# Releasing GpSimd's weight splits at VectorE's peak reductions, and moving weight blocks, transposes and small scale operations in a two-layer adaLN and FFN kernel

## The chip, the cores and the metric

One Trainium2 chip (trn2), one of its cores. The metric is the device time of one execution, in microseconds (us), lower is better. The engines are TensorE (PE in the views), VectorE (DVE), ScalarE (ACT), GpSimd (POOL) and SyncE (SP), which here only issues DMAs.

## The reference

The input `x` has 16 batches of 128 x 128 floats. Two layers are added to it, each a conditioning followed by an FFN. Cut to what matters:

```
# layer 0, conditioning: one 128x128 matrix for each batch, applied to x
w = scale * weight * y[:, None, :];  w = w * rsqrt(sum(w*w) + 1e-8);  c = einsum('boi,bil->bol', w, E)
# layer 0, FFN with quantised activations (each act_qdq needs the largest absolute value of its whole tensor)
act_qdq(x): s = max(max|x| / 32767, 1e-12);  clip(round(x / s), ...) * s
x = act_qdq(c);  up = act_qdq(x @ dq(w_up).T);  gate = act_qdq(x @ dq(w_gate).T)
sig = fixed_qdq_u16(sigmoid(gate));  gate = act_qdq(gate * sig);  o = act_qdq(gate * up);  return o @ dq(w_down).T
# layer 1, conditioning: a recurrence over 128 time steps
next_h = tanh(x_t @ Wx + b + prev_h @ Wh)
# layer 1, FFN: 8 experts of 512 hidden units with exact gelu, the best 2 of them mixed by a softmax
```

The two layers follow each other, so layer 1 cannot start before layer 0 has its result.

## The kernel before

The program is written by hand: each engine has its own list of instructions, and semaphores tie the lists together. Nothing is scheduled by a planner; the order in the source is the order on the engine.

**Front, up to about 82 us.** VectorE and ScalarE turn five tensors into integers. Each tensor's scale is made by `peak_to_scale(i, ...)`, i from 0 to 4: c, gate, up, gate times sigmoid, and the product o. VectorE first reduces pieces of the tensor to peaks (`block_peak`, `peak_gate_up`), then these to one column (`pk1`, semaphore `pk_part`). TensorE spreads that column over all partitions (`spread_peak`, a matmul with the identity into bank 7, semaphore `pk_all`). VectorE takes the maximum (`pkm`), the reciprocal and the scale (semaphore `scale_done`). While the spread runs, VectorE prepares the scale's limits: `unit` writes column 0 of `sc`, L708 writes it divided by QMAX, and L709 divided by TINY; then it does what the argument `meanwhile` names.

- The sigmoid stage (L825 to L833) works in six pieces of 1024 columns. ScalarE quantises a piece of gate (L596), takes the sigmoid (L600), and from the third piece on rounds it to 16 bits (L603); VectorE rounds the first two itself (`round_sigmoid`, L810), multiplies (L829, semaphore `g2_done`) and reduces (L723).
- The product stage (L836 to L845) has six pieces too. VectorE quantises the first (L836), ScalarE the others (L614, semaphore `g2q`) and up in three parts (L607, `upq`). VectorE multiplies (L841, `p_done`) and reduces (L723).
- `take_xT` on ScalarE evicts the transposes of `x` that TensorE makes at L1074.

**The experts' weights** are 16 chunks of 128 x 512 floats (`W_CHUNKS`). Each has to be scaled, split into a high and a low half-precision part, and transposed. The first `W_POOL` = 8 are split by GpSimd (`split_weights`, L375 to L377: scale, high part, difference), and SyncE transposes both parts by DMA (L335). For the other 8, ScalarE writes the high part (`weight_hi`, L535) and SyncE transposes it (L338), while TensorE makes the low part: for each chunk a **weight block** of four pairs of matmuls (L1092 to L1095) that ScalarE evicts (`weight_lo`, L540). There are eight chunk buffers for 16 chunks, so chunk 8 and later ones wait for the first eight transposes (semaphore `wt_t[0]`). GpSimd also dequantises the three FFN weights (`scale_weights`, L384 to L387), and splits the router weights, the recurrence's bias, the experts' second bias (`split_b2`) and Wh (`split_wh`).

`keep_busy(WARM)` gives TensorE 14 matmuls whose result nobody reads, ahead of the weight blocks. The spread for scale 4 stands ahead of the last two blocks (L1086).

**Middle, about 82 to 98 us.** `quantise_o` on VectorE, the down projection in five column chunks (`WIDTHS`) on TensorE, and the first 16 recurrence steps.

**Experts, about 98 us to the end.** TensorE runs the expert matmuls and the rest of the recurrence between them, chunk by chunk. `input_part` prepares `x_t @ Wx` for the next chunk's steps. The bias `b` enters in one of two ways: before chunk `BIAS_FROM` = 2 by one more matmul (`bh_rows` x `ones`), from that chunk on as the bias operand of the tanh (L663 to L666). Chunks 2 and 3 take two tanh for each step, chunk 2 in 32 steps and chunk 3 in 24.

## Time and profile before

| | |
|---|---|
| median of 3 executions | 293.2 us (292.99 to 293.34) |
| the profiled execution, its own time | 293.86 us |
| its span, first to last instruction | 292.1 us |
| busy: PE / DVE / ACT / POOL | 258.1 / 257.5 / 218.5 / 91.9 us |
| mean granted TensorE clock | 0.953 of full speed |

How to read it: the span is counted from the first instruction and leaves out 1.8 us around it. Every duration used below comes from this one profiled execution. Two engines have nearly the same busy time, so the shares of the whole say little; the stages have to be read one by one.

### The profile page before, as it was taken

What the parts mean: (1) busy time and instruction counts of PE and PEld (TensorE: products, weight loads), DVE (VectorE), ACT (ScalarE), POOL (GpSimd) and SP (SyncE); (2) the same over time, 40 slices, a digit from 0 to 9 for tenths busy, and PEclk for the clock granted to TensorE, in tenths of its full rate; (3) what the DMA queues carried; (4) which work ended last, traced back from release to release, by engine and by line L of the source; (5) the groups of instructions that cost most, each with busy time, mean ns of one, the idle gap of its engine ahead of it and who ended that gap; (6) DMA issues with size and microseconds to landing.
All of it is one profiled execution on the core that took longest, in us unless ns stands there. A gap on an engine that the chain in (4) does not pass through costs nothing.

```text
span 292.1 us, 7662 instructions
## 1 busy us (share of the span) xinstructions
PE 258.1 (88%) x2828; PEld 196.1 (67%) x2828; DVE 257.5 (88%) x638; ACT 218.5 (75%) x510; POOL 91.9 (31%) x181
## 2 busy tenths in 40 slices
PE   4999850039999999999999999999999999999994
PEld 3843450016866889888888676767677777778774
DVE  4899999989999999979988799778799988899885
ACT  5487899998742677777777777787678777788992
POOL 3539999250036413113212213333211232201000
PEclk9999957558999999999999999999999999999999
DMA  6992343001400000000000000000001000001001
GB/s 172 325 333 47 72 95 72 15 0 36 92 18 2 1 2 2 3 0 21 2 0 3 2 5 25 2 2 3 1 2 38 3 0 2 3 2 37 0 2 29
DMA packets 24041, 10.77 MB, mean 37 GB/s; under 512 B 13355, under 2 KB 22982, under 8 KB 24006
## 3 DMA queue, kind: packets, MB, share of 16 engines
q1 hardware_dynamic: 23470, 10.05, 13.7%
q8 instruction: 22, 0.36, 0.6%
q10 hardware_dynamic: 536, 0.26, 0.3%
q14 instruction: 13, 0.11, 0.1%
HBM read 6.11 MB, written 1.05 MB: 25 GB/s over the span
## 4 chain that ended last, share of the span: by engine, by line
PE 69%; DVE 24%; DMA 3%; issue 2%; ACT 1%; POOL 0%; SPq 0%; DVEq 0%
PE bank L998 68%; DVE peak L723 6%; DVE peak L805 4%; DVE big L829 3%; DVE big L841 3%; DMA wn<-in_w_gate 2%; DVE q L795 1%; DVE big L810 1%; DMA y_sb<-in_cond 1%; PE bank L1124 1%; DVE ws L750 1%; DVE big L836 1%; DVE big L849 1%; DVE big L977 0%; DVE pkm L712 0%
## 5 line engine op out<-in xcount | busy, mean ns | idle before, releaser
L998 PE MATMUL bank<-big,wt 128*128 128x384 f16 (+2 forms) x480 | 123.1, 336 | 0.0
L998 PE MATMUL bank<-wt,big 128*128 128x128 f16 (+1 forms) x1536 | 110.8, 219 | 0.2 <-DVE big L977 0.2
L998 PEld LDWEIGHTS bank<-wt,big 128*128 128x128 f16 x1536 | 98.2, 97 | 15.9 <-DVE big L977 0.5
L977 DVE TENSOR_TENSOR big<-big 128x384 f16<-128x384 f32 (+2 forms) x160 | 93.1, 587 | 17.7 <-ACT big L679 13.2
L677 ACT ACTIVATE big<-bank,miscT 128x384 f32<-128x384 f32 (+2 forms) x160 | 96.5, 604 | 10.3 <-PE bank L998 9.4
L998 PEld LDWEIGHTS bank<-big,wt 128*128 128x128 f16 (+1 forms) x480 | 44.8, 107 | 3.8 <-issue 0.2
L459 POOL TENSOR_TENSOR big<-q,big 128x16 f16<-128x16 f32 x56 | 23.5, 419 | 66.6 <-ACT q L666 66.6
L973 DVE CAST big<-big 128x512 f16<-128x512 f32 (+2 forms) x104 | 38.7, 372 | 4.0 <-ACT big L677 3.5
L932 DVE SCALAR_TENSOR_TENSOR wyT<-bank,gates,wyT 128x128 f32<-128x128 f32 x128 | 39.7, 343 | 0.3 <-issue 0.2
L679 ACT ACTIVATE big<-bank,miscT 128x384 f16<-128x384 f32 (+2 forms) x56 | 33.1, 592 | 0.0
L665 ACT ACTIVATE big<-bank,miscT 128x16 f16<-128x16 f32 x56 | 15.4, 276 | 18.1 <-PE bank L998 17.9
L998 PEld LDWEIGHTS bank<-q,wxh 128*128 128x128 f32 x142 | 23.6, 190 | 5.1 <-ACT q L637 1.2
L998 PE MATMUL bank<-q,wxh 128*128 128x16 f32 x142 | 21.3, 226 | 0.3 <-ACT q L637 0.3
L450 POOL CAST big<-q 128x64 f16<-128x64 f32 x18 | 6.6, 367 | 47.2 <-ACT q L666 46.9
L998 PE MATMUL bank<-ident,pk 128*128 128x128 f32 x10 | 2.9, 383 | 20.4 <-DVE pk L706 20.4
L666 ACT ACTIVATE q<-bank 128x16 f32<-128x16 f32 x56 | 10.3, 184 | 12.9 <-PE bank L998 12.5
L998 PEld LDWEIGHTS bank<-big,wh_hi 128*128 128x128 f16 x112 | 10.0, 96 | 12.9 <-POOL big L459 9.4
L998 PEld LDWEIGHTS bank<-ident,pk 128*128 128x128 f32 x10 | 2.0, 237 | 21.9 <-DVE pk L706 16.8
L586 ACT ACTIVATE big<-bank 128x512 f32<-128x512 f32 x24 | 13.4, 612 | 2.6 <-PE bank L998 2.3
L998 PE MATMUL bank<-q,wT_hi 128*128 128x512 f16 x48 | 15.1, 380 | 0.1
L666 ACT ACTIVATE q<-bank,miscT 128x16 f32<-128x16 f32 x56 | 15.1, 270 | 0.0
L723 DVE TENSOR_REDUCE peak<-big 128x1 f32<-128x1024 f32 x12 | 14.6, 1220 | 0.4
(177 smaller groups left out, 386.1 us busy)
## 6 DMA issues: line engine op xcount, KB each, us to landing
wnat<-in_w SPq DMA_DIRECT2D x8, 512.0 KB, 7.6
x_sb<-in_x SPq DMA_DIRECT2D x4, 256.0 KB, 4.1
out_block<-wyT SPq DMA_DIRECT2D x15, 64.0 KB
wn<-in_w_gate ACTq DMA_DIRECT2D x1, 192.0 KB, 5.4
wn<-in_w_up SPq DMA_DIRECT2D x1, 192.0 KB, 5.5
wn<-in_w_down SPq DMA_DIRECT2D x1, 192.0 KB, 5.5
b_in<-in_b SPq DMA_DIRECT2D x12, 4.0 KB
wt<-wyT SPq DMA_TRANSPOSE x8, 3.0
```

The source lines that it names most:

```text
L459: G.tensor_tensor(h_lo[:, at], h32[:, at], h_hi[:, at], ALU.subtract).then_inc(h_lo_done, 1)
L586: A(blk(t, j * NK + k), banks[GU_BANKS[n % 5]][:, :], ACT.Copy).then_inc(gu_sb, 1)
L665: A(h_hi[:, bass.ds(step * B, B)], sums, ACT.Tanh, bias=bias, scale=1 / WS).then_inc(h_hi_s, 1)
L666: A(h32[:, bass.ds(step * B, B)], sums, ACT.Tanh, bias=bias, scale=1 / WS).then_inc(h32_done, 1)
L677: A(g32[:, f, 0:w], ps_h[f][:, 0:w], ACT.Gelu, bias=bias, scale=1 / WS).then_inc(g32_done, 1)
L679: A(g_hi[:, s // NF, f, 0:w], ps_h[f][:, 0:w], ACT.Gelu, bias=bias, scale=1 / WS).then_inc(g_hi_done, 1)
L723: link(V.tensor_reduce(peak[:, i, n:n + 1], t, X, ALU.max, apply_absolute_value=True))
L805: link(V.tensor_reduce(peak[:, i, k:k + 1], tokens((gate2, up2)[i - 1], k), XY, ALU.max, apply_absolute_value=True))
L932: V.scalar_tensor_tensor(a, ps_y[par][:, P * j:P * (j + 1)], g, a, ALU.mult, ALU.add).then_inc(added, 1)
L973: V.tensor_copy(g_hi[:, par, f, 0:w], g32[:, f, 0:w]).then_inc(hi_v, 1)
L977: V.tensor_tensor(g_lo[:, par, f, 0:w], g32[:, f, 0:w], g_hi[:, par, f, 0:w], ALU.subtract).then_inc(g_lo_done, 1)
L998: return nc.tensor.matmul(o, l, r, start=start, stop=stop, skip_group_check=True)
```

## The change

Twelve edits in one. They are numbered here, and the prediction speaks of them by these names.

- **Limits.** `peak_to_scale` writes its two limits directly from two numbers (two operations instead of three), for scales 1, 3 and 4. Scale 0 takes them from a constant tile `limits` that GpSimd fills at the start, scale 2 from scale 1, both with no operation of VectorE.
- **Splits behind.** GpSimd's chunks 5, 6, 7 wait for VectorE's products: `split_behind(i, made, n)` starts after product n (n = 0: at once) and its last operation after product n+1. `scale_weights(1)` waits for `q_done`, the router weights for `g2_done` 6, the bias for `p_done` 1, `split_b2` for `p_done` 6 and its last operation for `pk_part` 5.
- **Two chunks moved.** Chunks 8 and 9 go from ScalarE and TensorE to GpSimd (`W_POOL` 10, `W_FIRST` 8), behind products 2 to 5 of the product stage; SyncE transposes them last, in full.
- **ScalarE's order.** Two quantised pieces before the table load, the others between weight parts; `low_byte(0)` ahead of the last two low parts.
- **Early transposes.** Two of the four transposes of `x` (8 of 16 matmuls, and 2 evictions) move to the start.
- **Spreads.** Spread 0 goes ahead of the transposes of the gate weights; spread 4 comes after the last weight block and two more warming matmuls. `WARM` 14 to 4, `START_WARM` 3 to 2.
- **wT_lo of down.** `weight_lo(2)` moves on VectorE from the peaks of up into the wait for spread 3.
- **upq.** Product n waits for the third of up that it reads, no longer for all three.
- **Bias.** `BIAS_FROM` 3: chunk 2's tanh has no bias operand, and chunk 1's `input_part` for those steps one more matmul of 512 columns.

```diff
-W_POOL = 8
+W_POOL = 10
+W_FIRST = 8
+X_EARLY = (6, 5)
+X_LATE = (1, 2)
-WARM = 14
+WARM = 4
+LATE_WARM = 2
-BIAS_FROM = 2
+BIAS_FROM = 3
-START_WARM = 3
+START_WARM = 2
...
+            def split_behind(i, made, n):
+                src, hi, lo = wnat[:, i % 2, i // 2, :], nat_of(i)[:, 0:FF], nat_of(i)[:, FF:2 * FF]
+                if n:
+                    pool.wait_ge(made, n)
+                link(G.tensor_scalar(src, src, WS, 0.0, ALU.mult, ALU.add))
+                link(G.tensor_scalar(hi, src, 1.0, 0.0, ALU.mult, ALU.add))
+                pool.wait_ge(made, n + 1)
+                G.tensor_tensor(lo, src, hi, ALU.subtract).then_inc(nat_done, 1)
...
+            pool.wait_ge(q_done, NK)
             scale_weights(1)
...
-            split_weights(POOL_FIRST, W_POOL)
+            split_weights(POOL_FIRST, W_FIRST - 3)
+            split_behind(W_FIRST - 3, g2_done, 0)
+            split_behind(W_FIRST - 2, g2_done, 2)
+            split_behind(W_FIRST - 1, g2_done, 4)
...
+            pool.wait_ge(wt_t[0], 16 * W_FIRST)
+            split_behind(W_FIRST, p_done, 2)
+            split_behind(W_FIRST + 1, p_done, 4)
             split_b2()
...
-                unit(sc[:, i, 0:1])
-                link(V.tensor_scalar(sc[:, i, 1:2], sc[:, i, 0:1], 1.0 / QMAX, None, ALU.mult))
-                link(V.tensor_scalar(sc[:, i, 5:6], sc[:, i, 0:1], 1.0 / TINY, None, ALU.mult))
+                for a, limit in enumerate((1.0 / QMAX, 1.0 / TINY) if unit else ()):
+                    link(V.tensor_scalar(sc[:, i, a:a + 1], unit[0], unit[1], limit, ALU.mult, ALU.mult))
...
-            dve.wait_ge(upq, NJ)
             for n in range(2 * NJ):
+                dve.wait_ge(upq, n // 2 + 1)
...
             for i in range(W_POOL, W_CHUNKS):
-                if i == W_CHUNKS - 2:
-                    spread_peak(4)
...
                 last.then_inc(w_lo_mm, 1)
+            keep_busy(LATE_WARM)
+            spread_peak(4)
```

How the order moves, at the two places on which the largest terms rest. First GpSimd from its sixth chunk (number 5) on, through the sigmoid and the product stage. `wnat` is a chunk as loaded, `nat` and `wyT` hold its two parts. Before:

```order
L375 TENSOR_SCALAR wnat<-wnat 128x512
L376 TENSOR_SCALAR nat<-wnat 128x512 [waits pool_step]
L377 TENSOR_TENSOR nat<-wnat,nat 128x512 [waits pool_step]
L406 TENSOR_SCALAR rw<-miscT 128x8 [waits misc_sb]
...
L421 TENSOR_SCALAR b2_in<-b2_in 96x512 [waits pk_part,ld_b2,bh_ready]
```

and now:

```order
L412 TENSOR_SCALAR wnat<-wnat 128x512 [waits g2_done]
L413 TENSOR_SCALAR nat<-wnat 128x512 [waits pool_step]
L415 TENSOR_TENSOR nat<-wnat,nat 128x512 [waits g2_done,pool_step]
L432 TENSOR_SCALAR rw<-miscT 128x8 [waits g2_done,misc_sb]
...
L412 TENSOR_SCALAR wnat<-wnat 128x512 [waits ld_w2,p_done,wt_t0,bh_ready]
L413 TENSOR_SCALAR wyT<-wnat 128x512 [waits pool_step]
L415 TENSOR_TENSOR wyT<-wnat,wyT 128x512 [waits p_done,pool_step]
...
L448 TENSOR_SCALAR b2_in<-b2_in 96x512 [waits p_done,ld_b2]
```

Each chunk's first and third operation now carry a wait for VectorE, and two chunks are new. Second, ScalarE in the product stage: `big<-big,sc` is a quantised piece, `xT` an evicted transpose, `wyT<-wnat` and `nat<-wnat` a high part, `wt<-bank` a low part. Before:

```order
L608 ACT_TABLE_LOAD
L546 ACTIVATE xT<-bank 128x512 [waits xT_mm] x2
L614 ACTIVATE big<-big,sc 128x1024 [waits scale_done]
...
L614 ACTIVATE big<-big,sc 128x1024 x3
L535 ACTIVATE wyT<-wnat 128x512 [waits ld_w2,wt_t0]
```

and now:

```order
L645 ACTIVATE big<-big,sc 128x1024 [waits scale_done]
L645 ACTIVATE big<-big,sc 128x1024
L649 ACT_TABLE_LOAD
L566 ACTIVATE wyT<-wnat 128x512 [waits ld_w2,wt_t0]
L566 ACTIVATE wyT<-wnat 128x512 [waits ld_w2]
L577 ACTIVATE xT<-bank 128x512 [waits xT_mm]
L645 ACTIVATE big<-big,sc 128x1024
L571 ACTIVATE wt<-bank 128x512 [waits w_lo_mm]
L566 ACTIVATE nat<-wnat 128x512 [waits ld_w3]
```

The first high part now precedes three of the five quantised pieces, and these stand behind low parts, which wait for TensorE.

## Rows read from the trace of the kernel before

**Rows 1.** Chain that ended last, in time: start, length, what.

```profile
166.53 121.80 PE bank L998 x1577
```

**Rows 2.** Timeline of VectorE, 19 to 27 us: start, length, line, operation, tiles.

```profile
19.41 1.86 DVE L795 SCALAR_TENSOR_TENSOR q<-c,q 128x512 f16<-128x512 f32 x2
...
26.17 0.56 DVE L763 TENSOR_TENSOR wT_lo<-bank,wT_hi 128x384 f16<-128x384 f32 x1
```

**Rows 3.** Timeline of GpSimd, 19 to 46 us.

```profile
22.32 0.84 POOL L387 TENSOR_TENSOR wn<-wn,ws 128x384 f32<-128x384 f32 x1
...
25.76 0.83 POOL L384 TENSOR_TENSOR wn<-wn,ws 128x384 f32<-128x384 f32 x1
...
27.87 0.83 POOL L387 TENSOR_TENSOR wn<-wn,ws 128x384 f32<-128x384 f32 x1
...
44.15 1.16 POOL L377 TENSOR_TENSOR nat<-wnat,nat 128x512 f16<-128x512 f32 x1
```

**Rows 4.** Timeline of VectorE, 39 to 57 us.

```profile
39.47 0.16 DVE L706 TENSOR_REDUCE pk<-peak 128x1 f32<-128x4 f32 x1
...
40.10 0.69 DVE L810 TENSOR_SCALAR big<-big 128x1024 f32<-128x1024 f32 x1
...
44.31 1.55 DVE L810 TENSOR_SCALAR big<-big 128x1024 f32<-128x1024 f32 x1
45.89 1.51 DVE L829 TENSOR_TENSOR big<-big 128x1024 f32<-128x1024 int16 x1
...
56.52 1.22 DVE L829 TENSOR_TENSOR big<-big 128x1024 f32<-128x1024 int16 x1
```

**Rows 5.** Timeline of VectorE, 59 to 79 us.

```profile
59.03 0.16 DVE L706 TENSOR_REDUCE pk<-peak 128x1 f32<-128x6 f32 x1
...
60.15 0.29 DVE L712 TENSOR_REDUCE pkm<-bank 128x1 f32<-128x128 f32 x1 [0.52 <-PE bank L998]
...
60.92 1.55 DVE L836 TENSOR_SCALAR big<-big,sc 128x1024 f32<-128x1024 f32 x1
...
77.72 0.16 DVE L706 TENSOR_REDUCE pk<-peak 128x1 f32<-128x6 f32 x1
...
78.53 0.29 DVE L712 TENSOR_REDUCE pkm<-bank 128x1 f32<-128x128 f32 x1 [0.21 <-PE bank L998]
```

**Rows 6.** Timeline of ScalarE, 53 to 72 us.

```profile
53.26 1.34 ACT L603 ACTIVATE big<-big 128x1024 uint16<-128x1024 f32 x1
...
60.24 1.28 ACT L608 ACT_TABLE_LOAD   x1
...
65.54 3.23 ACT L614 ACTIVATE big<-big,sc 128x1024 f32<-128x1024 f32 x3
68.66 1.15 ACT L535 ACTIVATE wyT<-wnat 128x512 f16<-128x512 f32 x2
...
70.92 0.60 ACT L540 ACTIVATE wt<-bank 128x512 f16<-128x512 f32 x1 [1.11 <-PE bank L998]
```

**Rows 7.** Timeline of TensorE, 63 to 73 us (first matmul of blocks 8 and 10).

```profile
63.79 5.42 PE L998 MATMUL bank<-wT_hi 128*128 128x512 f16 x14 [3.76 <-DVE big L841]
69.34 0.49 PE L998 MATMUL bank<-ident,wnat 128*128 128x128 f32 x2
...
72.09 0.49 PE L998 MATMUL bank<-ident,wnat 128*128 128x128 f32 x2
```

**Rows 8.** Busy times by stretch: PE, PEld, DVE, ACT, POOL, then the granted clock.

```profile
37.50:38.00 0.50, 0.00 (x0) 0.00 (x0) 0.50 (x2) 0.50 (x1) 0.42 (x2) 0.60 0.76 155
...
66.00:68.00 2.00, 2.00 (x6) 0.66 (x5) 1.93 (x3) 2.00 (x3) 0.00 (x0) 0.50 0.00 0
68.00:70.00 2.00, 1.87 (x10) 0.98 (x9) 1.97 (x2) 1.81 (x3) 0.00 (x0) 0.92 0.00 0
```

**Rows 9.** Costliest groups: one tanh of a step with and without bias operand.

```profile
L666 ACT ACTIVATE q<-bank 128x16 f32<-128x16 f32 x56 | 10.3, 184 | 12.9 <-PE bank L998 12.5
...
L666 ACT ACTIVATE q<-bank,miscT 128x16 f32<-128x16 f32 x56 | 15.1, 270 | 0.0
```

More of the change, by code:

```diff
@@ L110, in program @@
         pkm = sb("pkm", [P, 5])
-        sc = sb("sc", [P, 5, 6])
+        sc = sb("sc", [P, 5, 5])
+        limits = sb("limits", [P, 2])
         x1 = c32[:, :, :].rearrange("p b l -> p (b l)")
@@ L367, in _ @@
             G.tensor_scalar(minus16[:, :], ident[:, :], -1.0 / WS, 0.0, ALU.mult, ALU.add).then_inc(consts, 1)
+            link(G.memset(limits[:, 0:1], 1.0 / QMAX))
+            G.memset(limits[:, 1:2], 1.0 / TINY).then_inc(consts, 1)
             link(G.memset(ones[:, :], 1.0))
@@ L570, in take_weights @@
                   ACT.Copy).then_inc(wT_hi_done, 1)
+            for k in range(len(X_EARLY)):
+                take_xT(k)
             take_weights(0)
@@ L607, in _, with take_g2 @@
                 A(third(up2, n), third(up2, n), ACT.Copy, scale=sc[:, 2, 4:5], bias=MAGIC).then_inc(upq, 1)
-            nc.scalar.preload_act_table(ACT.Gelu)
-            for k in range(2):
-                take_xT(k)
-            act.wait_ge(scale_done, 4)
-            for n in range(1, 2 * NJ):
-                A(sixth(sig2, n), sixth(sig2, n), ACT.Copy, scale=sc[:, 3, 4:5], bias=MAGIC).then_inc(g2q, 1)
-                if n <= 2:
-                    take_xT(n + 1)
-            act.wait_ge(wt_t[0], 16 * W_POOL)
-            weight_hi(W_POOL)
-            for i in range(W_POOL, W_CHUNKS - 1):
-                weight_hi(i + 1)
+            act.wait_ge(scale_done, 4)
+            def take_g2(n):
+                A(sixth(sig2, n), sixth(sig2, n), ACT.Copy, scale=sc[:, 3, 4:5], bias=MAGIC).then_inc(g2q, 1)
+            take_g2(1)
+            take_g2(2)
+            nc.scalar.preload_act_table(ACT.Gelu)
+            act.wait_ge(wt_t[0], 16 * W_FIRST)
+            weight_hi(W_POOL)
+            weight_hi(W_POOL + 1)
+            take_xT(2)
+            take_g2(3)
+            weight_lo(W_POOL)
+            weight_hi(W_POOL + 2)
+            take_xT(3)
+            take_g2(4)
+            weight_lo(W_POOL + 1)
+            weight_hi(W_POOL + 3)
+            take_g2(5)
+            for i in range(W_POOL + 2, W_CHUNKS - 2):
                 weight_lo(i)
+                weight_hi(i + 2)
             def low_byte(c):
@@ L627, in _ @@
             low_byte(0)
-            weight_lo(W_CHUNKS - 1)
+            for i in range(W_CHUNKS - 2, W_CHUNKS):
+                weight_lo(i)
             for c in range(1, LOW_SCALAR):
@@ L700, in _, with limits_of @@
             V = nc.vector
+            def limits_of(i):
+                own = sc[:, 1 if i == 2 else i, 0:2] if i else limits[:, :]
+                return own[:, 0:1], own[:, 1:2]
             def peak_to_scale(i, n, unit, meanwhile=lambda: None):
                 V.tensor_reduce(pk1[:, i:i + 1], peak[:, i, 0:n], X, ALU.max).then_inc(pk_part, 1)
-                unit(sc[:, i, 0:1])
-                link(V.tensor_scalar(sc[:, i, 1:2], sc[:, i, 0:1], 1.0 / QMAX, None, ALU.mult))
-                link(V.tensor_scalar(sc[:, i, 5:6], sc[:, i, 0:1], 1.0 / TINY, None, ALU.mult))
+                for a, limit in enumerate((1.0 / QMAX, 1.0 / TINY) if unit else ()):
+                    link(V.tensor_scalar(sc[:, i, a:a + 1], unit[0], unit[1], limit, ALU.mult, ALU.mult))
+                most = limits_of(i)[1]
                 meanwhile()
@@ L817, in _ @@
                         weight_lo(1)
-                    if i == 2 and k == 2:
-                        weight_lo(2)
-                peak_to_scale(i, NK, lambda u: link(V.tensor_scalar(u, sc[:, 0, 2:3], 1.0 / WS, None, ALU.mult)),
-                              (lambda: peak_gate_up(2, 0)) if i == 1 else (lambda: round_sigmoid(0)))
+                peak_to_scale(i, NK, (sc[:, 0, 2:3], 1.0 / WS) if i == 1 else None, (lambda: peak_gate_up(2, 0)) if i == 1 else (lambda: round_sigmoid(0)))
                 if i == 1:
@@ L880, in _ @@
             make_x1(CH - 1)
-            dve.wait_ge(wt_t[1], 16 * (W_CHUNKS - W_POOL))
+            dve.wait_ge(wt_t[1], 16 * (W_CHUNKS - W_FIRST))
             for k in range(ACC_SCALAR[0]):
@@ L1037, in transpose_weights, with transpose_x @@
                 last.then_inc(wT_mm, 1)
+            def transpose_x(k):
+                bank = banks[(X_EARLY + X_LATE)[k]]
+                for b in range(4 * k, 4 * k + 4):
+                    last = nc.tensor.transpose(bank[:, P * (b % 4):P * (b % 4 + 1)], x_sb[:, b, :], ident[:, :])
+                last.then_inc(xT_mm, 1)
+            for k in range(len(X_EARLY)):
+                transpose_x(k)
             for k in range(NK):
@@ L1070, in _ @@
             spread_peak(2)
+            for k in range(len(X_EARLY), NK):
+                transpose_x(k)
+            spread_peak(3)
             pe.wait_ge(wT_done, 3)
-            for k in range(NK):
-                for b in range(4 * k, 4 * k + 4):
-                    last = nc.tensor.transpose(banks[1 + k][:, P * (b % 4):P * (b % 4 + 1)], x_sb[:, b, :], ident[:, :])
-                last.then_inc(xT_mm, 1)
-            spread_peak(3)
             def keep_busy(n):
```

45 lines of the change are left out of this document (27 added, 18 removed).

## The prediction

> **What bounds the kernel now.** I read the chain of waits in time first. Before 82 us it runs almost wholly through VectorE; the experts' part is TensorE without a gap that matters, its last piece alone 121.80 us [rows 1]. So what the front gives back should come through to the end, and what frees ScalarE or VectorE in the experts' part should not. The timelines by engine then show what VectorE pays in the front beyond its own work. Its product L829 takes 1.22 us when GpSimd is idle and 1.51 when it is not, and the rounding L810 takes 0.69 or 1.55 [rows 4]. The reader should see in GpSimd's row what stood in the way: a difference that ran from 44.15 for 1.16 us, over the start of L810 at 44.31 [rows 3, 4]. L836 is the same kind of operation as L810 and also takes 1.55 [rows 5]. ScalarE and TensorE must be read beside it, since little slack is left: ScalarE's last rounding of the sigmoid stage ends at 54.60 and VectorE uses it at 56.52 [rows 4, 6].
>
> **The change, part by part.** Times are places in the execution shown.
>
> *Start.* The limits of scale 0 cost VectorE nothing now, but TensorE has eight more transposes before the spread, so I expect 0.25 us, between 0 and 0.4. Holding `scale_weights(1)` back frees VectorE's two operations at L795: they took 1.86 us together, and 1.4 would be two at the length of an undisturbed one, so 0.4 more. But GpSimd then starts at about 20.7. Its four operations take 2.94 us undisturbed (25.76 to 28.70) and so end at 23.65, where they ended at 23.16 [rows 3]. The transposes, the eviction and `weight_lo(1)` all follow GpSimd: VectorE, early by 0.6, has to wait there, and L763 ends about 0.2 later than the old 26.73 [rows 2]. The whole gain of the start is spent on this wait. TensorE and ScalarE behind it start the sigmoid stage some 0.26 us late.
>
> *Scales 1 and 2.* One limit operation less before scale 1 gives 0.19, and `weight_lo(2)` leaves the peaks of up: 0.56 [rows 2]. L706 moves from 39.47 to about 38.94. Three limit operations for scale 2 go, but then the spread is what ends last: at half clock it is 0.96 from the end of L706 to L712 (59.19 to 60.15) [rows 5]. L712 comes at 38.94 + 0.16 + 0.96 = 40.06, where it came when L810 ended, 40.79 [rows 4]. That makes 0.7 in all so far.
>
> *Sigmoid stage.* L810 loses 1.55 - 0.69 = 0.86; of the first three L829, two lose 0.29 and one 0.20: 0.78 [rows 4]. VectorE alone would reach L706 at 59.03 - 0.7 - 1.64 = 56.7. It will not, because ScalarE's last piece comes at 54.60 + 0.26 = 54.86 [rows 6]; a product and a peak of 1.22 and two gaps of 0.02 follow, and L706 starts at 57.4. **The gain is capped at 1.65 us here.** GpSimd's three chunks fit: its difference of 1.16 lies beside a peak of 1.22, and two scalings of 0.62 each overhang the peak by about 0.1.
>
> The Trainium skill (SBUF — State Buffer, Who interferes with whom) says of VectorE and GpSimd that the second to issue is fully blocked until the first ends. By that rule L810 would have ended at 45.31 + 0.69 = 46.00; the row has 45.86, so the trace agrees within 0.14. By the rule an overhang of 0.1 costs 0.1, which changes the sum by less than 0.3 over all pieces.
>
> *Scale 3 and L836.* `weight_lo(2)` (0.56) and two limit operations (0.37) fit exactly into the 0.96 of the spread; I cost them at nothing, and at 0.1 if the spread is fast. L836 loses 0.86 because `split_b2` is now behind the products. The product stage starts 1.65 + 0.86 = 2.5 us early, and VectorE alone would have L706 at 77.72 - 2.5 = 75.2 [rows 5].
>
> *ScalarE's chain in the product stage.* This is where I expect the bound. ScalarE's three L607 start when the sigmoid stage ends there, and so end at 60.24 + 0.26 = 60.50. Until the last high part it has five pieces at 1.04 (65.54 to 68.66 is three), a table load of 1.28, six high parts, four low parts and two xT, each 0.57 (two take 1.15) [rows 6]. The sum is 13.3 us. To this comes one wait: block 10 starts with the first high part at 64.4, and TensorE is then at half clock. A block takes 1.37 at full clock (69.34 to 72.09 is two) [rows 7], 2.75 at half: it ends at 67.2, and ScalarE is there at 66.6. So the last high part ends at 60.5 + 13.3 + 0.6 = 74.4. Its block takes 1.4 and the two warming matmuls 0.4, half of 0.39 (14 in 5.42 us [rows 7]) for each. TensorE is free at 76.2, and VectorE's peaks have been ready since 75.4. From the end of L706 to L712 it was 0.65 at full clock (77.88 to 78.53) [rows 5]: L712 comes at 76.8, **1.7 us early**. The pieces for VectorE are in time: the third is ready at 66.6 and wanted at 67.7, the fourth at 69.9 and 70.2, the fifth at 72.1 and 72.7.
>
> The clock rows carry this. It rose at 68.3, 4.5 us after the warming began at 63.79 [rows 7, 8]. Steady work from 64.4 on would bring it by 69, in block 11. If it rises earlier, ScalarE's wait of 0.6 goes. If it stays low for one block more, 0.5 is lost.
>
> *After L712.* The split of Wh (a cast and a difference of 128 columns) now follows `split_b2` at 76.6 and ends before VectorE's first `quantise_o` at 77.6: nothing, at most 0.7 if the scale comes earlier. SyncE's two late transposes are issued by 78 and needed at 83. Nothing else between 78.5 and the experts changes.
>
> *Experts.* A tanh without bias operand takes 184 ns, with it 270 [rows 9]. ScalarE is spared 64 x 86 ns = 5.5 us; I cost that at nothing, because TensorE is the chain there. The extra matmul of 512 columns is on TensorE: 0.2 us lost.
>
> **Sum.** -1.7 + 0.2 = -1.5 us. The profiled execution of 293.86 would become 292.4. The median shown is 0.7 lower than that execution, so the forecast for the median is 293.2 - 1.5 = **291.7 us**. Its own range, by the bounds of the start (0.4), the overhangs (0.3) and the block (0.6), is 290.9 to 292.4.
>
> **Rivals.**
>
> - *The clock comes early and VectorE holds the end.* The last spread then waits for L706 only: L712 at 75.4 + 0.65 = 76.05, 2.5 us early. But `quantise_o` would then meet the split of Wh and give back 0.3 to 0.7. Result -1.8 to -2.0 with the bias, 291.3. For it: the four warming matmuls run just ahead of the blocks. Against it: ScalarE's sum of 13.3 us alone ends at 73.8, which puts the last spread's start at 75.6. Chance 0.17.
> - *Slower: the clock falls behind the last spread.* Now TensorE has two blocks between the spread and the down projection; after the change it has nothing from 77.4 until the first `o_hi` at 78.8, then 1.3 us of work and another gap. It fell at 37.6, with TensorE idle since gate and up [rows 8]. If the matmuls from 81 us on start at half clock, it may last as long as the low stretch from 63.79 to 68.3, 4.5 us [rows 7, 8], in which half the work is done: 2.3 us lost, against 1.5 won, 0.8 slower than before, 294.0. A dip half as long gives 292.9. It decides from the point where the granted clock is 0.5 at the down projection's second chunk. Chance 0.1, half of it for the long dip.
> - *The queue behind GpSimd costs more.* A wait for a product's semaphore delays chunk 5 to 7, these delay `wt_t[0]`, and the first high part waits for it; or the clock rises a block later. Nothing in the rows shows a delay over 1 us. The gain falls to 0.6: 292.6. Chance 0.1.
> - *The table load is paid in full.* Today ScalarE has slack there; after the change the load is inside its chain, with work queued behind. If the switch holds the engine for twice the 1.28 of its row [rows 6], the gain falls by 1.3 us to 0.2: 293.0. Against it: the transposes' eviction followed this load at once. The Trainium skill (ScalarE: Activation LUTs, What ACT_TABLE_LOAD costs) states a drain of 1.38 us beside a load of 1.28. By that rule the time would be 293.1; the row shows the 1.28 and no drain. Chance 0.04.
> - *Nothing is released.* The splits could already lie beside the peaks. The rows say no: three L829, L810 and L836 are all stretched. Chance 0.02.
> - The remaining 0.57 is the forecast.
>
> **Numbers.** About 0.2% (0.6 us) is what a measurement of this kernel can tell from no change: below 292.6 is faster, above 293.8 slower. The forecast and the first rival are faster, 0.74, and a third of the rest adds 0.05: **faster 0.79**. The queue, the table load, the short dip and no release fall mostly within: **same 0.13**. The long dip, with a little for a cost that I don't see: **slower 0.08**. The range leaves out the long dip and reaches to the short one and to the first rival's lower end: 290.6 to 293.1.
>
> **What would show it right or wrong.** In the changed profile the products of the sigmoid stage should take 1.22 each and L810 and L836 0.69. There should be a new wait of VectorE for `weight_lo(1)` of about 0.8, and one for ScalarE's last sigmoid piece. L706 of scale 3 should start near 57.4, the last spread's L712 near 76.8 with TensorE, not VectorE, as what it waits for, and the clock should be at full speed from 69 on. Wrong would be: full clock before 66; a granted clock of 0.5 anywhere between 77 and 90; L712 later than 78; or an experts' part (from the first expert matmul to the end) that differs by more than 0.4 us from that of before.

## The result and the profile after

The changed kernel took **291.07 us**, the median of five executions (289.96 to 291.83), against 293.03 for the kernel before in the same comparison. The ratio is 0.9923, with a 95% interval from 0.9909 to 0.9937. The forecast was 291.7 us. Four of the five executions show a mean granted clock of TensorE of 0.941; the fifth, of 289.96, shows 0.953. That difference matters below.

| | before | after |
|---|---|---|
| profiled execution | 293.86 us | 291.07 us |
| its span | 292.1 us | 289.3 us |
| mean granted clock | 0.953 | 0.941 |
| first expert matmul | 105.89 | 104.24 |
| from there to the end of the chain's last long piece | 182.44 | 181.23 |

The chain that ended last, with the page's shares by engine first, then start, length, what:

```profile
PE 78%; ACT 13%; DVE 4%; issue 2%; POOL 1%; DMA 1%; SPq 0%; DVEq 0%; POOLq 0%
```

```profile
53.86 4.46 ACT big L640 x3
...
63.56 2.84 PE bank L1045 x12
...
72.16 3.54 PE bank L1045 x28
...
77.93 6.02 PE bank L1045 x32
...
104.24 181.23 PE bank L1045 x2344
```

VectorE has nearly left the chain. In the whole view it goes through ScalarE from 32.64 on, through all of the sigmoid stage, and from 62.88 on to and fro between ScalarE and TensorE through the weight blocks. The experts' part is one piece, where it was several [rows 1]. The timeline of VectorE in the changed kernel (start, length, line, operation, tiles, and in brackets the idle time before it and what ended that):

```profile
18.36 1.22 DVE L845 SCALAR_TENSOR_TENSOR q<-c,q 128x512 f16<-128x512 f32 x2
...
25.44 0.56 DVE L812 TENSOR_TENSOR wT_lo<-bank,wT_hi 128x384 f16<-128x384 f32 x1 [1.04 <-ACT wT_hi L600]
...
38.09 0.16 DVE L755 TENSOR_REDUCE pk<-peak 128x1 f32<-128x4 f32 x1
...
39.20 0.29 DVE L761 TENSOR_REDUCE pkm<-bank 128x1 f32<-128x128 f32 x1 [0.21 <-PE bank L1045]
...
42.65 0.69 DVE L860 TENSOR_SCALAR big<-big 128x1024 f32<-128x1024 f32 x1
43.38 1.23 DVE L876 TENSOR_TENSOR big<-big 128x1024 f32<-128x1024 int16 x1
...
53.96 1.23 DVE L876 TENSOR_TENSOR big<-big 128x1024 f32<-128x1024 int16 x1 [0.57 <-ACT big L636]
...
56.48 0.16 DVE L755 TENSOR_REDUCE pk<-peak 128x1 f32<-128x6 f32 x1
...
57.52 0.29 DVE L761 TENSOR_REDUCE pkm<-bank 128x1 f32<-128x128 f32 x1
...
58.30 0.75 DVE L883 TENSOR_SCALAR big<-big,sc 128x1024 f32<-128x1024 f32 x1
...
74.37 0.16 DVE L755 TENSOR_REDUCE pk<-peak 128x1 f32<-128x6 f32 x1
...
75.80 0.29 DVE L761 TENSOR_REDUCE pkm<-bank 128x1 f32<-128x128 f32 x1 [0.90 <-PE bank L1045]
```

Line by line these answer to [rows 2, 4, 5]: the pair of L845 1.22 instead of 1.86, the rounding of the sigmoid stage 0.69 instead of 1.55, the product behind it 1.23 instead of 1.51, L883 0.75 instead of 1.55. Two waits are new: 0.57 for ScalarE's last sigmoid piece, and 0.90 for TensorE at the last spread. GpSimd, ScalarE and TensorE in the same kernel, from their timelines:

```profile
19.67 0.83 POOL L393 TENSOR_TENSOR wn<-wn,ws 128x384 f32<-128x384 f32 x1 [5.67 <-DVE q L845]
```

```profile
61.59 1.28 ACT L649 ACT_TABLE_LOAD   x1
62.88 1.15 ACT L566 ACTIVATE wyT<-wnat 128x512 f16<-128x512 f32 x2
...
66.42 0.60 ACT L571 ACTIVATE wt<-bank 128x512 f16<-128x512 f32 x1 [0.87 <-PE bank L1045]
...
72.46 0.65 ACT L566 ACTIVATE nat<-wnat 128x512 f16<-128x512 f32 x1
```

```profile
77.93 0.49 PE L1045 MATMUL bank<-big,wT_hi 128*128 128x256 f16 x3 [2.24 <-DVE big L898]
```

TensorE stood still for 2.24 us behind the last spread. The busy times by stretch show what came of it (the stretch and its length; the busy time of PE, PEld, which is TensorE's weight loads, DVE, ACT and POOL, with the number of instructions; then the granted clock, where 0.50 is 1.2 GHz and 1.00 is 2.4 GHz; the last two columns are DMA):

```profile
68.00:70.00 2.00, 1.92 (x17) 1.65 (x15) 1.93 (x3) 2.00 (x5) 1.24 (x2) 0.98 0.33 66
...
78.00:80.00 2.00, 2.00 (x12) 1.50 (x12) 1.68 (x3) 2.00 (x4) 0.00 (x0) 0.58 0.89 167
80.00:82.00 2.00, 2.00 (x9) 1.02 (x8) 1.59 (x4) 0.15 (x1) 0.00 (x0) 0.57 0.00 0
82.00:84.00 2.00, 1.94 (x15) 1.18 (x12) 1.97 (x3) 0.21 (x2) 1.24 (x1) 1.00 0.00 0
```

The clock rose at 68.1, as expected, and fell again from about 78.3 to 81.7, in the middle of the down projection.

**Where the time went.** The five L761 (L712 before) cut the execution into stretches that don't depend on when the first load landed. That landing varies from one execution to the next: the first load of the profiled execution of before ended at 3.35, that of after at 2.89, which alone is 0.46 of the difference between the two. All numbers are differences of start times in one profiled execution of each kernel; the last column is the median of all its timed executions, with its ratio to before, which was timed again beside each group of runs (293.03 to 293.45). So kernels of different groups are compared by their ratios.

| kernel | scale 0 to 2 | 2 to 3 | 3 to 4 | scale 4 to first expert matmul | experts | median us (ratio) |
|---|---|---|---|---|---|---|
| before | 25.48 | 19.44 | 18.38 | 27.36 | 182.44 | 293.03 |
| after | 25.02 | 18.32 | 18.28 | 28.44 | 181.23 | 291.07 (0.9923) |
| b_bias3 | 25.46 | 19.45 | 18.38 | 27.37 | 181.36 | 292.38 (0.9960) |
| a_bias2 | 24.71 | 18.67 | 18.29 | 27.37 | 182.33 | 291.36 (0.9940) |
| a_fill | 24.70 | 18.63 | 18.30 | 27.36 | 181.22 | 290.10 (0.9886) |
| a_nowaits | 25.01 | 18.79 | 18.24 | 28.40 | 181.24 | 291.45 (0.9928) |
| b_behind | 25.47 | 17.83 | 21.11 | 27.38 | 182.44 | 293.71 (1.0019) |
| b_behind_warm | 25.48 | 17.82 | 19.57 | 27.37 | 182.43 | 292.62 (0.9976) |
| a_last1 | 24.71 | 18.65 | 17.65 | 27.44 | 181.23 | 289.60 (0.9871) |
| a_early | 25.01 | 18.33 | 17.65 | 28.57 | 181.22 | 291.05 (0.9924) |
| a_noq | 24.69 | 18.32 | 18.28 | 28.44 | 181.21 | 291.16 (0.9920) |
| a_last1_nowaits | 24.71 | 19.11 | 18.26 | 28.10 | 181.23 | 291.20 (0.9928) |
| a_last1_early | 25.01 | 18.33 | 17.96 | 27.77 | 181.22 | 289.70 (0.9872) |
| a_ops | 25.29 | 18.05 | 18.29 | 28.50 | 181.23 | 291.58 (0.9934) |

From before to after: -1.68 from scale 0 to scale 4 (63.30 to 61.62), +1.08 behind it, -1.21 in the experts' part. Ahead of scale 0, L755 to L761 is 0.81 (13.37 to 14.18), where it was 1.18: -0.37. The sum is -2.18; the medians differ by 1.96. The forecast had -1.7 for the front, scale 0 included, nothing for the stretch behind it, and +0.2 for the experts.

### The profile page after: what moved, and what is told of

It is laid out like the page before. It is cut to its first block, busy times and chain, and to the rows that moved or that the text cites. A ratio compares the mean times of both kernels' runs of the same rounds, so it can differ in the third digit from the quotient of the medians.

```text
span 289.3 us, 7599 instructions
## 1 busy us (share of the span) xinstructions
PE 253.0 (87%) x2795; PEld 194.5 (67%) x2795; DVE 253.9 (88%) x629; ACT 213.0 (74%) x506; POOL 91.7 (32%) x189
## 4 chain that ended last, share of the span: by engine, by line
PE 78%; ACT 13%; DVE 4%; issue 2%; POOL 1%; DMA 1%; SPq 0%; DVEq 0%; POOLq 0%
PE bank L1045 76%; ACT big L633 2%; ACT big L629 2%; ACT big L636 2%; ACT big L640 2%; ACT big L645 1%; DVE q L845 1%; PE bank L1179 1%; PE bank L1098 1%; DMA y_sb<-in_cond 1%; ACT big L619 1%; ACT wt L571 1%; ACT nat L566 1%; DVE big L1024 1%; ACT L649 0%
## 5 line engine op out<-in xcount | busy, mean ns | idle before, releaser
L490 POOL TENSOR_TENSOR big<-q,big 128x16 f16<-128x16 f32 x56 | 24.4, 436 | 64.2 <-ACT q L710 64.2
L710 ACT ACTIVATE q<-bank 128x16 f32<-128x16 f32 x88 | 16.0, 182 | 12.7 <-PE bank L1045 12.5
L709 ACT ACTIVATE big<-bank 128x16 f16<-128x16 f32 x32 | 5.9, 184 | 12.9 <-PE bank L1045 12.9
L855 DVE TENSOR_REDUCE peak<-big 128x1 f32<-128x1536 f32 x8 | 14.0, 1744 | 0.2
```

Source lines behind the costliest of these rows:

```text
L490: G.tensor_tensor(h_lo[:, at], h32[:, at], h_hi[:, at], ALU.subtract).then_inc(h_lo_done, 1)
L710: A(h32[:, bass.ds(step * B, B)], sums, ACT.Tanh, bias=bias, scale=1 / WS).then_inc(h32_done, 1)
L855: link(V.tensor_reduce(peak[:, i, k:k + 1], tokens((gate2, up2)[i - 1], k), XY, ALU.max, apply_absolute_value=True))
```

## The experiments

Every kernel is an edit of the one before or of the changed one.

**The bias operand, both ways.** a_bias2 puts it back into the changed kernel, b_bias3 takes it out of the one before.

```
-BIAS_FROM = 3
+BIAS_FROM = 2      # a_bias2; b_bias3 is 2 -> 3 in the kernel before
```

> The change with the bias operand put back in chunk 2, nothing else. Theory A, the step chain: in the experts' part of before TensorE stood 1.2 us at about 162.6 and 1.2 us at about 165.3, each ended by ScalarE's tanh and GpSimd's split of a state; the tanh without its bias operand frees ScalarE there, and this is the 1.2 us that the experts' part lost (182.48 to 181.26). Then this kernel is 1.0 to 1.4 us slower than the change, 292.3, with stalls of TensorE of about 1.2 us back some 60 us into the experts' part, and the experts' part is 182.5 again. Theory B, as forecast: TensorE is the chain, the bias is worth nothing, the matmul spared gives 0.2: 0.2 us faster than the change, 290.9, and the experts' part stays at 181.1. Theory C: the experts' part is shorter because the front hands over in another order; then also within 0.2 of the change.

> The kernel before with the bias operand taken from chunk 2, nothing else. Theory A (step chain): 1.0 to 1.4 us faster than before, 291.8, all of it after the first expert matmul. Theory B (forecast): 0.2 us slower, 293.2. Theory C (order of the handover): within 0.2 of before. If A holds, the front of the change alone is worth only about 0.7 us of the 1.96 at the end.

Measured: 291.36 (ratio 0.994, 0.9919 to 0.9961) and 292.38 (0.996, 0.9946 to 0.9974). Theory A holds in its size: the operand is the cause of the 1.2 us. The experts' part is 182.33 with it in the changed kernel and 181.36 without it in the kernel before. The theory's reading of where the 1.2 us lie, as two stops of TensorE, does not hold. The medians say the same for b_bias3, 1.07 below before's 293.45. For a_bias2 the median alone is only 0.3 above the change's, since four of its seven executions escaped the fall of the clock (0.945 to 0.953, 290.69 to 291.36) and three did not (0.940 to 0.941, 292.00 to 292.89). The chain of the kernel before, around the place (start, length, what):

```profile
162.75 0.28 ACT q L666
...
163.09 0.62 POOL big L459
...
165.83 0.66 POOL big L459
```

Twice the chain leaves TensorE for a recurrent step: a tanh for the high half, one for the full state, then GpSimd's difference, 1.2 us each time (162.56 to 163.76). TensorE does not stand still for these 1.2 us. Its timeline has other matmuls beside them, and the step's matmul at 163.76 starts 0.65 after the pair of 512 columns ahead of it, where such a pair takes 0.44 when nothing waits. The chain's hop is long, and what it costs is 0.2.

The timelines of a_bias2 and of the changed kernel can be laid side by side, matmul by matmul, with times counted from the first expert matmul. At the first input matmul behind the extra one, a_bias2 is 0.41 ahead (53.53 against 53.94): this is the price of the extra matmul. Behind the second hop it is 0.07 ahead (60.50 against 60.57), so the two hops together are worth 0.34. At 203.62 in its timeline it is 1.11 behind (100.21 against 99.10), and stays there. Most of the loss, 1.18, thus comes in 24 us of the long piece that the chain shows as unbroken TensorE. The weight loads (PEld) show what it is, first in a_bias2, then in the changed kernel:

```profile
163.91 0.10 PEld L1045 LDWEIGHTS bank<-big,wh_hi 128*128 128x128 f16 x1 [0.58 <-POOL big L490]
...
179.97 0.10 PEld L1045 LDWEIGHTS bank<-big,wh_hi 128*128 128x128 f16 x1 [0.48 <-POOL big L490]
...
203.61 0.10 PEld L1045 LDWEIGHTS bank<-big,wh_hi 128*128 128x128 f16 x1 [0.48 <-POOL big L490]
```

```profile
182.06 0.10 PEld L1045 LDWEIGHTS bank<-big,wh_hi 128*128 128x128 f16 x1 [0.31 <-POOL big L490]
...
201.88 0.10 PEld L1045 LDWEIGHTS bank<-big,wh_hi 128*128 128x128 f16 x1 [0.29 <-POOL big L490]
```

From 179.97 to 203.61 a_bias2 has nine weight loads that wait 0.39 to 0.48 for GpSimd's difference, and its matmuls fall behind by 0.07 to 0.20 at each of them. In the changed kernel no wait between 178 and 203 is longer than 0.31. The view of L459 (L490) by who waited for it adds the waits up, in us and times, before and after:

```profile
  PEld bank L998: 9.4, 27
```

```profile
  PEld bank L1045: 5.0, 17
```

Of these 4.4 us, about 1.5 reach the end. The kernel before and b_bias3, laid side by side, differ in the same way: 0.41 for the extra matmul, 0.34 at the two hops, 1.14 behind them.

**Filling TensorE's gap behind the last spread.** a_fill:

```
             keep_busy(LATE_WARM)
             spread_peak(4)
+            keep_busy(9)
```

> The change with nine warming matmuls behind the last spread, on TensorE's idle time from 75.7 to 77.9. Theory D: the granted clock falls at 78.3 because TensorE stands still behind the last spread, and the half clock from 78.3 to 81.7 costs 1.1 us (the spread's L712 was 2.7 us early, the first step only 1.66). Nine matmuls of 0.22 fill 1.9 of the 2.2 us, the clock stays full, and the kernel is 1.0 to 1.2 us faster than the change, 290.0, with a mean granted clock of 0.953 instead of 0.941. Rival E: the gain is lost elsewhere between the spread and the first step (the low bytes, VectorE's quantise and x1), and the clock dip lies beside waits: then 0 to 0.3 faster, with full clock throughout.

Measured: 290.10 (ratio 0.9886, 0.9866 to 0.9907). Theory D holds: scale 4 to the first expert matmul is 27.36, not 28.44, which is before's own 27.36. Only the mean clock was put too high (0.944 to 0.947), because in these executions it rose later, at about 70. Busy times by stretch of a_fill, columns as above:

```profile
78.00:79.00 1.00, 0.80 (x8) 0.75 (x9) 0.93 (x4) 1.00 (x3) 0.00 (x0) 1.00 0.97 185
...
80.00:81.00 1.00, 0.93 (x6) 0.60 (x7) 0.93 (x4) 0.41 (x1) 0.00 (x0) 1.00 0.00 1
```

So the fall costs 1.08 us. That is less than half of the 3.4 us from its fall to its rise. Probably part of it lies beside VectorE's own work, which no run shows alone.

The profiled execution of a_bias2 tells the fall from the gap. It has no filling and the same gap, but its clock stayed at full speed:

```profile
78.18 0.49 PE L1045 MATMUL bank<-big,wT_hi 128*128 128x256 f16 x3 [2.25 <-DVE big L898]
```

From scale 4 to the first expert matmul it takes 27.37. So the gap by itself costs nothing, and the fall of the clock is the whole 1.08.

**The last block behind the last spread.** a_last1:

```
+            for i in range(W_POOL, W_CHUNKS - 1):
+                weight_block(i)
-            keep_busy(LATE_WARM)
             spread_peak(4)
+            weight_block(W_CHUNKS - 1)
+            keep_busy(LATE_WARM)
```

> The change with the last spread ahead of the last weight block (and of the two late warming matmuls), not behind it. Theory J: the blocks ahead of the last spread cost twice: the spread waits for TensorE (L761 at 75.80 with 0.90 idle, L755 had been at 74.37), and behind it TensorE stands still for 2.2 us, which lets the clock fall for 1.07 us of loss. With one block behind the spread, L761 comes 0.65 after L755, 0.8 earlier; the block fills the gap, and the clock stays full: scale 3 to 4 falls from 18.29 to 17.5, last spread to first expert matmul from 28.44 to 27.4; the kernel is 1.6 to 1.9 us faster than the change, 289.3. Rival K: the block behind the spread delays the down projection or the low bytes, or the clock falls all the same: 0 to 0.8 faster.

Measured: 289.60 (ratio 0.9871, 0.9856 to 0.9885). Theory J, by 0.3 less than the expected 289.3. TensorE and VectorE of a_last1, from their timelines:

```profile
74.81 0.49 PE L1045 MATMUL bank<-ident,pk 128*128 128x128 f32 x2 [0.84 <-DVE pk L755]
...
77.67 0.49 PE L1045 MATMUL bank<-big,wT_hi 128*128 128x256 f16 x3 [0.66 <-DVE big L898]
```

```profile
75.41 0.29 DVE L761 TENSOR_REDUCE pkm<-bank 128x1 f32<-128x128 f32 x1 [0.28 <-PE bank L1045]
```

The spread now waits for VectorE's peak. The gap behind it is 0.66 instead of 2.24, and the clock stays at 1.00 there. This part of the change, the blocks ahead of the last spread, goes one block too far: with the last one behind it the front is 0.63 shorter and the fall of the clock is gone.

**The clock ahead of the blocks.** a_early:

```
-WARM = 4
+WARM = 14
-            pe.wait_ge(p_done, 1)
             keep_busy(WARM)
```

> The change with fourteen warming matmuls instead of four, started without the wait for the first product, so from 57.4 on. Theory L: the clock is at full speed before block 10 (at 63.5), the block takes 1.4 instead of 2.84, ScalarE's wait of 0.87 for it goes, and with it scale 3 to 4 falls by 0.6 to 0.8, to 17.6: 0.6 to 0.8 faster if the clock dip behind the last spread stays, 290.4. Rival M: the clock falls again between the warming and the blocks, or the blocks' high parts, not block 10, set the last spread: then 18.1 to 18.3 and no gain; or the warming runs at half clock into block 10 and delays it: up to 0.5 slower.

Measured: 291.05 (ratio 0.9924, 0.9907 to 0.9941), so no gain in all. Theory L is right on its own stretch, 17.65, with block 10 at full clock and ScalarE's wait of 0.87 gone. The last spread comes 0.6 earlier, TensorE then stands still for 2.37, the clock falls, and scale 4 to the first expert matmul is 28.57. By these stretches the kernel should still be 0.5 faster than the change, and the median doesn't show it. Its six executions lie in two groups, 290.52 to 290.71, with the profiled one, and 291.38 to 291.85. What the second group lost is open: no trace of it was kept.

**Both, and why they don't add.** a_last1_early has the two edits together.

> a_last1 with fourteen warming matmuls from the end of the spread of scale 3 on, without the wait for the first product. a_early and a_last1 both brought scale 3 to 4 to 17.65, each alone. Theory S: 17.65 is VectorE's own length (six products, six peaks, a rounding), so the two together give nothing more: 17.6 to 17.7, within 0.2 us of a_last1, 289.6. Rival T: each took off a part of the same chain, and together they give 0.3 to 0.6 more.

Measured: 289.70 (ratio 0.9872, 0.9858 to 0.9887), within 0.2 of a_last1 as theory S has it, but not for its reason alone. 3 to 4 is 17.96 and not 17.65. The blocks end so early that TensorE now stands still *ahead* of the spread; its timeline, and the stretch behind:

```profile
74.24 0.79 PE L1045 MATMUL bank<-ident,pk 128*128 128x128 f32 x2 [1.85 <-DVE pk L755]
```

```profile
75.00:76.00 1.00, 1.00 (x8) 0.87 (x6) 0.75 (x4) 0.00 (x0) 0.86 (x3) 0.50 1.02 188
```

The clock falls at the spread, which runs at half clock (L761 waits 0.59 instead of 0.28).

**GpSimd's waits taken out again.** a_nowaits, on the changed kernel; a_last1_nowaits is the same edit on a_last1:

```
             def split_behind(i, made, n):
...
-                if n:
-                    pool.wait_ge(made, n)
...
-                pool.wait_ge(made, n + 1)
...
-            pool.wait_ge(g2_done, 6)
...
-            pool.wait_ge(p_done, 1)
...
-                pool.wait_ge(p_done, 6)
+                pool.wait_ge(pk_part, 4)
...
-                pool.wait_ge(pk_part, 5)
```

> The change without the waits that hold GpSimd's splits behind products and peaks (those for g2_done, p_done and pk_part in front of weight chunks 5 to 9, the router's, the bias and the b2 splits); the moved blocks, limits and waits of the first scales stay. Theory F, as forecast: VectorE's L860 goes back to 1.55 and up to three L876 to 1.5, which with ScalarE's cap costs about 1 us at the scale 3 (L755 from 56.5 to 57.5), and the product stage runs with splits beside it; since ScalarE's chain to the last high part starts with scale 3, the last spread is about 1 us later and the kernel 0.6 to 1.2 slower than the change, 291.9. Rival G: ScalarE and TensorE hold the end of the front in any case and the table load, high parts and blocks take what is lost: within 0.3 of the change, 291.1, though L860 and L876 are stretched.

Measured: 291.45 (ratio 0.9928, 0.9913 to 0.9944). Between F and G, nearer to G: scale 0 to 4 is 62.04, 0.42 more, and the medians can't tell the two apart. VectorE and GpSimd of a_nowaits:

```profile
43.14 1.51 DVE L870 TENSOR_TENSOR big<-big 128x1024 f32<-128x1024 int16 x1
...
58.51 0.98 DVE L877 TENSOR_SCALAR big<-big,sc 128x1024 f32<-128x1024 f32 x1
```

```profile
39.95 2.02 POOL L412 TENSOR_TENSOR nat<-wnat,nat 128x512 f16<-128x512 f32 x1
```

F was wrong on the rounding: L854 took 0.74 here, since GpSimd's queue stood elsewhere. Four products are stretched all the same (1.51, 1.39, 1.51, 1.48). Their excess over 1.22 is 1.0 us in the sigmoid stage; the stretch grows by 0.47 only, because ScalarE held it at 18.32. GpSimd pays too: its difference of 1.16 took 2.02. The Trainium skill (SBUF — State Buffer, Who interferes with whom) says the later one of the two is blocked until the first ends. By it the difference would have ended 1.16 after VectorE's product at 40.95, so at 42.11; the row has 41.97, and the trace agrees within 0.14.

> The best kernel so far (a_last1, the last block behind the last spread) without the waits that hold GpSimd behind VectorE. On the change itself they were worth 0.4 of the front (scale 0 to 4 62.04 against 61.62), because the last spread waited for TensorE. Theory Q: in a_last1 VectorE holds the product stage (17.65), so now the stretch of L877 and of the products comes through: scale 3 to 4 18.24, scale 0 to 4 62.04 against 61.01, 1.0 us slower than a_last1, 290.6. Rival R: the waits are worth as little as on the change: 0 to 0.4 slower, 289.8.

Measured: 291.20 (ratio 0.9928, 0.9906 to 0.9949), 1.6 us above a_last1, with intervals that don't meet. Theory Q, and more. 3 to 4 is 18.26, and scale 0 to 4 is 62.08 against 61.01. The other 0.6 is the clock again (28.10): with VectorE late, TensorE stands still ahead of the spread, as its timeline and the stretch behind show.

```profile
75.48 0.49 PE L1039 MATMUL bank<-ident,pk 128*128 128x128 f32 x2 [1.90 <-DVE pk L749]
```

```profile
77.00:78.00 1.00, 1.00 (x6) 0.70 (x5) 0.97 (x3) 0.49 (x1) 0.00 (x0) 0.50 1.10 205
```

So the worth of the waits depends on which engine holds the stretch behind them: 0.4 us in the change, 1.6 in a_last1.

**Only GpSimd's waits, in the kernel before.** b_behind, with `split_b2` behind the second and third product; b_behind_warm has WARM at 21 on top:

```
-            split_weights(POOL_FIRST, W_POOL)
+            split_weights(POOL_FIRST, W_POOL - 3)
+            split_behind(W_POOL - 3, g2_done, 0)
+            split_behind(W_POOL - 2, g2_done, 2)
+            split_behind(W_POOL - 1, g2_done, 4)
...
+            pool.wait_ge(g2_done, 6)
...
+            pool.wait_ge(p_done, 1)
...
-                pool.wait_ge(pk_part, 4)
+                pool.wait_ge(p_done, 2)
...
+                pool.wait_ge(p_done, 3)
```

> The kernel before with only GpSimd held back: its last three weight splits, the router's, the bias and the b2 splits wait for VectorE's products. Stretches are from L712 of one scale to L712 of the next. Theory H: in before VectorE is the chain up to the last spread (two weight blocks still stand behind the spread there), so what the release frees comes through: the sigmoid stage (scale 2 to 3) falls from 19.44 to about 18.4, the product stage (scale 3 to 4) from 18.38 to 17.5, 1.9 us in all, median 291.5: as much as the whole change gained, and more than the change's own front. Rival I: the product stage is bound by ScalarE and TensorE at 18.3 in before too, as in the change: then only the sigmoid stage gains, 0.4 to 1.1, median 292.4 to 293.0.

Measured: 293.71 (ratio 1.0019, 0.9991 to 1.0048): no gain, and both H and I are wrong. The median hides two groups, though: six of the twelve executions took 292.36 to 293.22, with a mean clock of 0.956 to 0.957, and six 294.19 to 296.31, with 0.941 to 0.953. The profiled one (294.75) is of the second group. In it the sigmoid stage gained 1.61, more than H had, and the product stage lost 2.73. TensorE and VectorE of b_behind, then its busy times by stretch:

```profile
69.10 0.49 PE L1016 MATMUL bank<-ident,wnat 128*128 128x128 f32 x2 [1.60 <-ACT wyT L553]
```

```profile
79.41 0.29 DVE L730 TENSOR_REDUCE pkm<-bank 128x1 f32<-128x128 f32 x1 [2.66 <-PE bank L1016]
```

```profile
70.00:72.00 2.00, 2.00 (x14) 1.87 (x14) 1.97 (x2) 1.12 (x2) 0.43 (x1) 0.69 0.54 109
72.00:74.00 2.00, 2.00 (x12) 1.78 (x10) 1.93 (x3) 0.98 (x2) 0.00 (x0) 0.50 0.44 88
```

The warming starts with the first product, so it too is early; it ends 1.60 before ScalarE has the first high part, and the clock falls inside the blocks (at 70.75, in the second). ScalarE gave that high part at the same place as before, as its own work sets it. Six blocks stand ahead of the spread, and VectorE waits 2.66 for it.

> The kernel with only GpSimd held back (b_behind), with 21 warming matmuls instead of 14, so that TensorE has no gap of 1.6 us before its first weight block. In b_behind the sigmoid stage gained 1.6 us and the last spread still came 1.0 later than in before (scale 3 to 4: 21.11), because the clock fell inside the first block, and six blocks stand ahead of the spread. Theory O: without the dip the six blocks end 8.4 us after they begin (69.1 to 77.5), as in before, so scale 3 to 4 is 19.8: scale 0 to 4 is 63.1, against 63.3 in before. The release by itself is worth 0 to 0.3 us, median 293.2, since ScalarE, which is bound by its own work in both stages, starts the weight highs where it did. Rival P: blocks and spread follow VectorE: scale 0 to 4 at 61.5, median 291.5.

Measured: 292.62 (ratio 0.9976, 0.9962 to 0.9990). Theory O, a little low: 3 to 4 is 19.57, scale 0 to 4 is 62.87 against 63.30 of before. Undisturbed by the clock, the release, here with seven more warming matmuls, is worth 0.4 in the front of the old kernel. The faster six of b_behind's executions, with a median of 292.68, lie at the same place. The rest of the change's 1.68 comes with its other parts, ScalarE's high parts and TensorE's blocks brought forward above all; that share is argued from the chain, since no kernel had these parts alone.

**The wait ahead of the second `scale_weights`.** a_noq:

```
-            pool.wait_ge(q_done, NK)
             scale_weights(1)
```

> The change without GpSimd's wait for VectorE's q before the second scale_weights. The record said: the wait frees 0.4 us on VectorE and takes as much again behind it, through TensorE's transposes of the weights and weight_lo(1). Then the second of the two L845 takes 1.3 again instead of 0.7, the wait of 1.04 before weight_lo(1) goes, and scale 0 to scale 2 stays within 0.2 of 24.7 to 25.0: the kernel within 0.2 us of the change. Rival N: the wait costs more than it frees: scale 0 to 2 falls by 0.4 to 0.8 and the kernel is as much faster.

Measured: 291.16 (ratio 0.9920, 0.9904 to 0.9936), the same as the change. VectorE and GpSimd:

```profile
18.59 1.86 DVE L844 SCALAR_TENSOR_TENSOR q<-c,q 128x512 f16<-128x512 f32 x2
```

```profile
18.75 1.14 POOL L393 TENSOR_TENSOR wn<-wn,ws 128x384 f32<-128x384 f32 x1 [4.99 <-DVE ws L805]
```

The pair takes 1.86 again and the wait of 1.04 is gone, as expected. Scale 0 to 3 is 43.01 against 43.34: this wait costs the change 0.33 us there, which no median resolves. That it gains nothing is shown.

**Three column operations put back.** a_ops:

```
+                for _ in range(3 if i in (0, 2) else 0):
+                    link(V.tensor_scalar(sc[:, i, 2:3], limits[:, 0:1], 1.0, None, ALU.mult))
                 most = limits_of(i)[1]
```

> The change with three one-column operations of about 0.18 us put back on VectorE between peak and scale, for scale 0 and for scale 2, where the change took them away. They write a column that is overwritten later. Theory U, as forecast: at scale 0 they are on the path: 0.35 to 0.45 later there (L755 to L761 0.81 becomes 1.2). At scale 2 they lie within the 0.96 of the spread at half clock: nothing there. The kernel is 0.4 us slower than the change, with the cost entirely before scale 0. Rival V: ScalarE's chain, which holds the sigmoid stage, takes in the delay of scale 0 as well: no change.

Measured: 291.58 (ratio 0.9934, 0.9918 to 0.9949). From the start of L755 to that of the maximum (L763 in this kernel) it is 1.21 at scale 0 (13.66 to 14.87), against 0.81. At scale 2 the operations were not quite hidden:

```profile
38.85 0.52 DVE L759 TENSOR_SCALAR sc<-limits 128x1 f32<-128x1 f32 x3
...
40.16 0.27 DVE L763 TENSOR_REDUCE pkm<-bank 128x1 f32<-128x128 f32 x1
```

From L755 to L763 is 1.38, where the change has 1.11. But scale 0 to 3 is 43.34, to the hundredth that of the change. The 0.27 lost at scale 2 is taken in behind it, where ScalarE holds the stage. U holds for scale 0, and V for scale 2.

## Why the prediction was right, and where it was not

- **Start: right.** L755 to L761 shrank by 0.37, within the 0 to 0.4 given for 0.25. The pair of L845 took 1.22 for the 1.4 assumed. The new wait for `weight_lo(1)` was 1.04 for about 0.8, and the delay of ScalarE's sigmoid stage, put at 0.26, is 0.33 by a_noq.
- **Scale 2: right.** L761 waits for the spread (0.21), as "the spread is what ends last" had it.
- **Sigmoid stage: right.** L860 and L876 fell to 0.69 and 1.23, and the gain was capped by ScalarE, with a wait of 0.57 for its last piece. VectorE alone is at 17.83 in b_behind. In the change and the seven kernels made from it in which the splits are held back, scale 0 to 3 is 43.0 to 43.4.
- **Last spread: right.** From scale 0, put at 14.98 (15.23 less 0.25), to 76.8 it was to be 61.8; it is 61.62. TensorE, not VectorE, was what L761 waited for. From ScalarE's last L640 to its last high part I had 13.3 and a wait of 0.6; 59.49 to 73.11 is 13.6, with a wait of 0.87.
- **"After L712 nothing": wrong.** The rival "the clock falls behind the last spread" came true in its short form, which had half of a chance of 0.1. It is in the trace of the profiled execution, and by the mean clock of 0.941 in four of the five. The step that failed was weighing it as unlikely. The mechanism and the place were named; the gap, expected from 77.4 to 78.8, was put too short: TensorE is free at 75.68, 0.1 ahead of L761 and not 0.6 behind it, and has nothing until 77.93. It cost 1.08, near the 1.1 of that form.
- **"Experts: I cost that at nothing, because TensorE is the chain there": wrong.** The tanh without its operand is worth 1.5, and the extra matmul cost 0.41 and not 0.2; together they give the 1.2. The sentence was read off the last long piece [rows 1], which is shown as TensorE without a break. But TensorE waits inside it, for weights that come from ScalarE's tanh through GpSimd: 1.2 of the 1.5 lie in nine waits of 0.39 to 0.48 in there, and 0.3 at the two places ahead of it, 162.6 and 165.3, where the whole view shows the chain leave TensorE.
- **So the total, 0.63 below the forecast, hides two errors of opposite sign**: 1.08 too little loss behind the spread, 1.4 too little gain in the experts' part (+0.2 for -1.2), and 0.3 of gain in the front. That the total came out so near is luck in this part. The front, from scale 0 to scale 4, was forecast on its mechanism. Both signs named as "would be wrong" did appear: a granted clock of 0.5 between 77 and 90, and an experts' part that differs by more than 0.4.
- **The table load: right.** It is inside ScalarE's chain now and took its 1.28; L566 follows at 62.88, 0.01 behind it. The Trainium skill (ScalarE: Activation LUTs, What ACT_TABLE_LOAD costs) states a drain of 1.38 beside it. The row shows none, and the measurement decides here.

## What to carry to other kernels

When an edit makes one engine early, look at once for who now stands still, ahead of the hand-over and behind it: here the clock fell behind most of the gaps of TensorE of 1.6 to 2.4 us, and each fall gave back 0.3 to 1.5 us. One real block of work moved into the gap (a_last1) was worth more than warming. "TensorE is the chain" has to be checked inside the long pieces too: the chain view shows a piece as unbroken although the weight loads in it wait, and nine waits of under 0.5 us cost 1.2 us here. And removing contention pays only as far as the next engine's own sum, so much the same waits were worth 0.4 us in two kernels, 1.6 us in a third, and nothing in the median where the clock fell behind them.
